# Output rows stored in one transfer behind the last load, and the last chunk's loads re-cut, in a graph aggregation with layer norm

## The reference

```
keep   = (u >= 0.1)
x_drop = x * keep / 0.9
y      = x + matmul(adj, x_drop)
out    = (y - mean(y)) / sqrt(var(y) + 1e-5)      # over the 64 columns of a row
```

## Time and profile before

| | |
|---|---|
| median of the runs shown | 648.54 us |
| the profiled execution | 648.75 us, span 647.0 us |
| DMA | 274.77 MB, 425 GB/s on average |
| PE | busy 519.4 us, 80% of the span |
| DVE, ACT | busy 52.5 us and 17.9 us |
| granted TensorE clock, mean | 0.938 |

### The profile page before, as it was taken

One profiled execution on the slowest core, in us unless ns is written; L12 is line 12 of the kernel. 1 busy time (PEld: TensorE's weight loads), 2 busy tenths in 40 slices (PEclk: granted clock), 3 DMA queues, 4 the chain that ended last, 5 costly groups with the idle time before them and its releaser, 6 DMA issues.

```text
span 647.0 us, 4980 instructions
## 1 busy us (share of the span) xinstructions
PE 519.4 (80%) x2184; PEld 173.9 (27%) x2184; DVE 52.5 (8%) x97; ACT 17.9 (3%) x45; POOL 1.3 (0%) x11
## 2 busy tenths in 40 slices
PE   0397889878887889788977798898788797888897
PEld 0122323222222322222222232222223232232324
DVE  1930101010010100101001010100101001010100
ACT  0000200000000000000000000000000000000001
POOL 0000000000000000000000000000000000000000
PEclk9998889898988979897989798998989798998999
DMA  9999999999999999999999999999999999999994
GB/s 390 428 434 431 436 435 432 427 434 431 440 401 446 438 425 442 426 433 434 425 442 434 425 431 444 420 447 421 441 435 418 451 434 433 435 432 424 429 419 185
DMA packets 8643, 274.77 MB, mean 425 GB/s; under 512 B 960, under 2 KB 1088, under 8 KB 1984
## 3 DMA queue, kind: packets, MB, share of 16 engines
q1 hardware_dynamic: 8064, 272.76, 97.9%
q10 hardware_dynamic: 576, 1.97, 0.7%
HBM read 272.63 MB, written 2.10 MB: 425 GB/s over the span
## 4 chain that ended last, share of the span: by engine, by line
DMA 70%; PE 27%; another core or an unknown queue 1%; issue 0%; SPq 0%; ACT 0%; DVE 0%
DMA piece<-adj 67%; PE acc L150 27%; DMA piece<-adj_last 3%; SPq L109 0%; ACT squares L234 0%; ACT sums_T L231 0%; SPq L105 0%; DVE rows L296 0%; SPq L104 0%; ACT std L237 0%; DVE rstd L294 0%
## 5 line engine op out<-in xcount | busy, mean ns | idle before, releaser
L150 PE MATMUL acc<-piece,xdrop 128*64 128x512 f32 x2048 | 501.0, 635 | 112.2 <-DMA piece<-adj 111.4
L150 PEld LDWEIGHTS acc<-piece,xdrop 128*64 128x64 f32 x2048 | 157.5, 146 | 443.5 <-issue 298.2
L274 DVE SCALAR_TENSOR_TENSOR y<-folded,x_sb 128x256 f32<-128x256 f32 x15 | 6.4, 425 | 540.0 <-PE folded L165 540.0
L165 PE MATMUL folded<-fold,sums_T 128*128 128x64 f32 x120 | 16.6, 281 | 11.5 <-ACT sums_T L207 11.5
L207 ACT COPY sums_T<-acc 128x512 f32<-128x512 f32 x15 | 8.8, 586 | 493.5 <-PE acc L150 493.5
L165 PEld LDWEIGHTS folded<-fold,sums_T 128*128 128x128 f32 x120 | 14.5, 191 | 24.7 <-ACT sums_T L207 24.7
L285 DVE TENSOR_TENSOR rows<-y,rstd 128x256 f32 x15 | 6.4, 426 | 1.9
L278 DVE TENSOR_TENSOR squares<-y 128x256 f32<-128x256 f32 x15 | 6.4, 425 | 0.5
L281 DVE TENSOR_REDUCE square_sum<-squares 128x4 f32<-128x256 f32 x15 | 6.3, 420 | 0.5
L260 DVE SCALAR_TENSOR_TENSOR xdrop<-xdrop,x_sb 128x1024 f32<-128x1024 f32 x4 | 4.9, 1221 | 13.3 <-DMA xdrop<-u 13.3
L199 ACT ACTIVATE std<-square_sum,eps 128x4 f32<-128x4 f32 x15 | 4.5, 297 | 39.0 <-DVE square_sum L281 39.0
(11 more groups left out here) (17 smaller groups left out, 6.2 us busy)
## 6 DMA issues: line engine op xcount, KB each, us to landing
piece<-adj SPq DMA_DIRECT2D x30, 5376.0 KB, 28.9
piece<-adj SPq DMA_DIRECT2D x15, 5632.0 KB, 28.4
piece<-adj_last SPq DMA_DIRECT2D x1, 5120.0 KB, 27.8
piece<-adj_last SPq DMA_DIRECT2D x1, 3840.0 KB, 23.2
piece<-adj_last SPq DMA_DIRECT2D x1, 2816.0 KB, 19.1
x_sb<-x SPq DMA_DIRECT2D x1, 2048.0 KB, 7.6
xdrop<-u SPq DMA_DIRECT2D x1, 2048.0 KB, 12.0
piece<-adj_last SPq DMA_DIRECT2D x1, 2048.0 KB, 23.6
```

What stands on the lines that cost most here:

```text
L150: last = nc.tensor.matmul(acc[D * h:D * h + D, :], xdrop[:, k, :], piece[:, b0 + b, :], start=(k < 2), stop=(k >= NB - 2))
L165: last = nc.tensor.matmul(folded[:, j, :], sums_T[:, j * P:j * P + P], fold[:, :], start=True, stop=True)
L274: nc.vector.scalar_tensor_tensor(out=y[:, 0:nj, :], in0=folded[:, 0:nj, :], scalar=1.0 / KEEP, in1=x_sb[:, bass.ds(block0, nj), :], op0=AL ...
```

## The change

Two things are changed. First, ACT issues no stores any more. In their place SP issues one store of 60 of the 64 row groups, 1920 KB, behind the last chunk's eight loads and ahead of the last store, on the queue that the loads use. It waits for the rows of chunk 14 (`rows_ready`, 15), and SP then waits at its end for both stores. ACT's code becomes one loop over chunks 1 to 14. One wait is added on ACT in the tail (`rstd_ready`, 15), which stands for the order that the stores gave before. Second, the last chunk's table of loads is 18, 13, 10, 7, 6, 4, 4, 2 blocks in place of 20, 15, 11, 8, 5, 2, 2, 1.

```
-PARTS = ((0, 0, 20), (1, 0, 15), (2, 0, 11), (2, 11, 8), (1, 15, 5), (0, 20, 2), (2, 19, 2), (1, 20, 1))
+PARTS = ((0, 0, 18), (1, 0, 13), (2, 0, 10), (2, 10, 7), (1, 13, 6), (0, 18, 4), (2, 17, 4), (1, 19, 2))
@@ block.sync
                 sp.dma_start(pieces[s][:, b:b + size, :], adj_last[0, :, k0:k0 + size, :]).then_inc(part_in[n], 16)
                 k0 += size
+            sp.wait_ge(rows_ready, FINAL)
+            sp.dma_start(out[:, 0:NB - J, :], rows[:, 0:NB - J, :]).then_inc(stored, 16)
             sp.wait_ge(rows_ready, FINAL + 1)
             sp.dma_start(out[:, NB - J:NB, :], rows[:, NB - J:NB, :]).then_inc(stored, 16)
+            sp.wait_ge(stored, 32)
@@ block.scalar
-            def store(c, first, blocks):
-                act.wait_ge(rows_ready, c + 1)
-                act.dma_start(out[:, bass.ds(first, blocks), :], rows[:, bass.ds(first, blocks), :]).then_inc(stored, 16)
             wide(0, again=False)
-            for c in range(1, GROUP):
+            with act.Fori(1, CHUNKS - 1) as c:
                 wide(c)
-            store(3, 0, GROUP * J)
-            with act.Fori(1, CHUNKS // GROUP - 1) as g:
-                for n in range(GROUP):
-                    wide(g * GROUP + n)
-                store(g * GROUP + (GROUP - 1), g * (GROUP * J), GROUP * J)
-            for n in range(GROUP - 1):
-                wide(CHUNKS - GROUP + n)
-            store(CHUNKS - 2, NB - GROUP * J, GROUP * J - J)
...
+            act.wait_ge(rstd_ready, FINAL)
             act.wait_ge(last_var, J)
             nc.scalar.activation(std[:, :], square_sum[:, :], ACT.Sqrt, bias=eps_lifted[:, :],
                                  scale=1.0 / D).then_inc(std_ready, 1)
-            act.wait_ge(stored, 16 * (CHUNKS // GROUP + 1))
```

More of the change, by code:

```diff
@@ L20 @@
 FINAL = CHUNKS - 1
-GROUP = 4
 QUARTERS = 4
```

## The result

The changed kernel takes 644.3 us, the median of 6 runs (643.69, 643.75, 643.99, 644.61, 644.69, 646.21), against 648.62 us before (6 runs, 648.3 to 648.76): a ratio of 0.9937, 95% interval 0.9923 to 0.9950. It is faster by 4.3 us. What was forecast is 643.8 us; the three best runs lie on it, and three lie 0.8 to 2.4 us above. The profiled execution is the slowest of the six, 646.21 us with a span of 644.4, and it shows what that one lost.

A forecast was written before the change was run, and what follows sets the result against it. The load stream was taken to bound the kernel: -4.50 us for removed stores, -0.2 for the load table and smoother end, 0 for the new store, together -4.7, from 648.54 to 643.84 us (predicted 643.8); range 643.0 to 646.0 us.

The forecast's parts named there:

- What bounds the kernel: Whole kernel: the load stream sets the time, 38.78 us per chunk without a store, while PE is busy 80%.
- The stores that go: ACT's stores during the load stream: three of 512 KB cost 1.20 us each, one of 384 KB 0.90; gain 4.50 us.
- check of the 384 KB store: Last chunk's third-load entry: expected 627.85, actual 628.86, later by about 0.9 us (0.04 its own delay), taken as that store's cost.
- The table of loads: Last chunk's load sizes: the new table and smoother end gain 0.1 to 0.2 us, bounded by 0 and 0.5.
- The store that comes: 1920 KB store behind the last load: takes 4.50 us, hidden behind the tail of PE, ACT and DVE, priced at 0.
- The cover: Tail after the last load: time to spare between the large store's data end and the last store's data, 1.1 to 2.8 us.
- Small edits: ACT's loop and added wait: 0, at most 0.1 us; SP waiting for the stores instead of ACT: -0.1 to +0.2 us.
- rival (a): Chunk 14's third piece: PE's clock falls to half, PE enters the last chunk late, 0.5 to 1.8 us more; chance 0.13.
- PE's slack: Last chunk: PE's time to spare shrinks from about 1.8 us to 0.9 us.
- (b): Kernel end: the large store holds up the last store, up to 1.8 us, giving 644.5 to 645.8 us; chance 0.13.
- (c): Kernel end: HBM writes are slow packet by packet, the large store takes 17.6 us, time 654.8 us; chance 0.04.
- (d): Load stream: the removed stores' 1.20 us come back as something else, such as a stretched beat; 648.5 us; chance 0.04.

The follow-up runs named there:

- the lift early: Changed kernel, its own eight loads, with chunk 14 written out so the four lift products stand between its second and third piece: median 643.95 us, ratio 0.9925.
- the tripled store: Changed kernel plus two more 1920 KB stores of the same rows to scratch HBM, between the large and last store on SP's queue: median 651.56 us.
- the 16 runs named above: Runs of the changed kernel (644.30 us), the new stores with the old load table (644.25), and the changed kernel without the large store (643.88).
- the ten with PE made late: Ten runs of the changed kernel with 16 unused matmuls on PE between the lift and the last chunk's first product: median 650.01 us.
- the kernels with unused products: Changed kernel with unused matmuls added on PE, before the last chunk or in PE's waits, to one or both partition halves: medians 643.75 to 689.46 us.
- nine loads: Changed kernel with lift products before chunk 14's third piece, nine last-chunk loads, and that chunk's waits filled with unused matmuls to both halves: median 643.75 us.

## Why the prediction was right

**What bounds the kernel.** Right. The beat without stores is 38.78 us everywhere, and chunk 14's third piece is entered 3.60 us earlier (600.01 to 596.41).

**The stores that go, 4.50 us.** Right. 3.60 us is seen in the beat; the last load lands at 635.5, forecast 635.4, against 640.0 before, so 0.9 went in the last chunk. The store on ACT's queue gives back 4.5 us at the seventh load, and with it the whole gain. The working's check of the 384 KB store has a small slip: 628.86 less 627.85 less 0.04 is 0.97 us, not 0.9; it changes nothing.

**The table of loads, 0.1 to 0.2 us.** Of the right kind, somewhat low: in the kernel before PE ends 0.36 us earlier by it in the profile and the median falls by 0.44, inside the bounds of 0 to 0.5. In the changed kernel the falls of the clock cover it (644.25 without, 644.30 with). What was right is that the seventh load bounds the end where PE is on time: with the lift early PE enters it at 634.19 and ends at 637.01 (forecast 634.2 and 637.25).

**The store that comes, 0.** Right. It lands at 640.1, forecast before 642; leaving it out gains 0.1 us at most. The cover was worked out as 1.1 to 2.8 us, and the tripled store leaves 1.2. The rule of the Trainium skill that a transfer costs 2.0 us and its bytes at 436 GB/s ("DMA: Bandwidth & Descriptors", "Anatomy of one DMA") was meant for another path and gave 6.5 us. Counted back from the landing by the windows' GB/s, 1.97 MB moved from about 633.3 on, so the store took at least 6.8 us by this estimate, and 97% of these bytes were through by 638, after 4.7 us. The trace agrees with the rule to 0.3 us for the landing, and with the 4.50 us of the prediction for the bulk.

**Small edits.** Nothing in the traces shows a cost of ACT's loop or of SP's wait for the stores. The added wait costs some 0.06 us: between ACT's last square and its root the chain has 0.03 us before (643.77 to 643.80) and 0.08 after (641.20 to 641.28), and from PE's end to the issue of the last store it is 2.89 us in place of 2.82. That is within the 0.1 us allowed.

**PE late through its clock, rival (a).** This is the mis-sized term. The sum and its likeliest case were 643.84 us, and the three short runs, by their times those in which chunk 14's third piece is clean, are at 643.69 to 643.99. But the median is 644.30, since half the runs are longer, the profiled one by PE's lateness and the other two, which have no trace, most likely by it too. Three numbers were off. The chance was set at 0.13, although 5 of 15 third pieces of before were long; the last two pieces being clean was given weight that one execution doesn't bear. Seven of the 16 runs named above and three of the ten with PE made late are of the long kind. PE's slack was put at 0.9 us and is 0.6 to 0.8: on time PE ends at 637.09 where without a wait it would be 636.3, 11.37 in place of 9.67 us, 1.70 more, moved its end by 1.0 (to 638.08), and 12.69, 3.02 more, by 2.3 (to 639.39). And the price was given as up to 1.8 us, where it is 2.4. One of six runs, 646.21, lies over the range's 646.0 for that. In the kernel before PE had more slack at the end: the prediction says 1.8 us, but its own numbers, 641.97 less 639.9, give 2.1, and by these a fall of 1.7 us would have cost nothing there. The change spent most of that slack by making the load stream faster.

**Rivals (b), (c) and (d).** (b) didn't occur: the last store still lands in 1.8 us. (c) is refuted by the tripled store, (d) by the beat. That the median of 644.3 still lies close to the forecast is in part luck: a seventh run of the short kind would have put it at 643.99, one of the long kind at 644.61.

## What to carry to other kernels

When the DMA engines are busy from end to end, a store in the middle costs its bytes at the loads' rate, even if nothing waits for it; put it behind the last load, where the compute tail covers it, and check that the cover is longer than the store. Use the same queue as the loads: issued on another queue while loads were waiting, the store took turns with them and the gain was gone. When a stream gets faster, look again at the engine that was just fast enough: here TensorE's slack fell under the cost of one fall of its clock, and moving 1 us of needed work into its last wait gave the slack back, and the spread went.

## What the runs showed of the hardware that was not expected

Float32 matmuls of 64 output partitions and 512 columns stand 0.21 us apart when they go in turn to the upper and the lower half of the partitions, and 0.43 us apart when all go to one half. The timelines of the kernels with unused products have both, first one half, then (nine loads) both halves:

```profile
582.10 4.88 PE L167 MATMUL spare<-xdrop 128*64 128x512 f32 x11
```
```profile
594.26 1.94 PE L168 MATMUL spare<-xdrop 128*64 128x512 f32 x8
```

The recorded duration of one has a median of 592 ns in both cases, so the duration doesn't show it; only the spacing does. Those to one half also all wrote the same values of the spare tile, and the runs don't tell whether the half or the repeated place sets the 0.43 us. The kernel's own products, by even and odd blocks, stand at the short spacing; had they the long one, PE's time on them would be about twice as long.
